# A four-layer graph network kernel: who keeps the block sums, who makes the spread matrix, and how GATv2's leaky logits are formed

## The reference, cut to what matters

```python
e = leaky_relu(xl[src] + xr[dst], 0.2)
logit = einsum('ehc,hc->eh', e, att)
a = exp(logit - segment_max(logit, dst)[dst])
out = segment_sum(a / segment_sum(a, dst)[dst] * xl[src], dst)
```

## Time and profile before

| | us |
|---|---|
| median of 3 runs | 8000.28 (7995.58 to 8005.35) |
| the profiled execution, its own time | 8003.79 |
| its span, first to last instruction | 8002.0 |
| sweep of GATv2, 128 wide (914 to 1566 us) | 652 |
| sweep of GATv2, 256 wide (1664 to 2487) | 823 |
| sweep of GAT (2670 to 3285) | 615 |
| three sweeps of the transformer | 682, 684, 682 |
| sweep of GIN (7106 to 7715) | 609 |

### The profile page before, as it was taken

How to read it: one execution, slowest core, us unless ns; L and a number is a source line. 1 busy time by engine, 2 the same in 40 slices (tenths; PEclk the granted TensorE clock), 3 DMA queues, 4 the chain that set the end, 5 groups by cost and what they waited for, 6 DMA issues and landing times. The chain is left out here.

```text
span 8002.0 us, 138934 instructions
## 1 busy us (share of the span) xinstructions
PE 5981.8 (75%) x30254; PEld 4761.3 (60%) x30255; DVE 5204.0 (65%) x17428; ACT 3151.4 (39%) x10642; POOL 3541.3 (44%) x3878
## 2 busy tenths in 40 slices
PE   2787577678886788497887897886887887937676
PEld 1665466657774566386665785665875665814455
DVE  7664488768887566538997328997338998353323
ACT  0111266646664466235553225553325553300015
POOL 0677366545552477306662006662006663037740
PEclk9999999899997688699998998998999998955678
DMA  1000211222222233326553026553026554023330
GB/s 29 3 3 3 55 48 48 39 74 73 72 74 40 79 102 102 62 101 187 175 177 84 2 94 185 176 174 96 0 89 180 176 177 104 0 82 100 101 68 16
DMA packets 306941, 689.93 MB, mean 86 GB/s; under 512 B 95900, under 2 KB 135510, under 8 KB 306390
## 3 DMA queue, kind: packets, MB, share of 16 engines
q0 software_dynamic: 209536, 581.61, 27.0%
q1 hardware_dynamic: 81264, 98.11, 3.8%
q10 hardware_dynamic: 15846, 7.19, 0.4%
HBM read 605.77 MB, written 80.89 MB: 86 GB/s over the span
## 5 line engine op out<-in xcount | busy, mean ns | idle before, releaser
L943 POOL DMA_INDIRECT arena<-tab_l,idx x2320 | 2203.7, 950 | 1032.6 <-issue 568.4
L1020 PE MATMUL bank<-arena,onehots 128*128 128x264 f32 (+3 forms) x6496 | 1980.6, 436 | 339.0 <-DVE onehots L852 189.4
L981 PE MATMUL bank<-arena,spreads 128*128 x5568 | 1458.6, 370 | 598.0 <-ACT spreads L1034 242.6
L1020 PEld LDWEIGHTS bank<-arena,onehots 128*128 128x128 f32 x6496 | 1312.1, 221 | 673.7 <-DVE onehots L852 211.9
L981 PEld LDWEIGHTS bank<-arena,spreads 128*128 128x128 f32 x5568 | 966.9, 206 | 827.7 <-issue 761.7
L1213 DVE TENSOR_TENSOR acc<-acc,bank 128x264 f32 (+3 forms) x1624 | 654.9, 403 | 498.2 <-PE bank L1020 486.7
L1034 ACT ACTIVATE spreads<-bank 128x256 f32<-128x256 f32 x1392 | 524.2, 377 | 900.6 <-PE bank L969 896.2
L1108 DVE TENSOR_TENSOR arena<-arena,bank 128x512 f32<-128x512 f32 x928 | 629.3, 680 | 265.9 <-ACT stats L1056 146.7
L861 ACT ACTIVATE onehots<-iota_row,slot_loc 128x128 f32<-128x128 f32 x1856 | 632.3, 391 | 28.6 <-PEq L1693 24.2
L943 POOL DMA_INDIRECT arena<-tab_l0b,idx x464 | 441.2, 951 | 374.9 <-ACT arena L1074 235.6
L930 POOL COPY idx<-slot_typed 128x16 int32 (+1 forms) x87 | 17.8, 204 | 1329.0 <-SPq L901 1328.6
(11 more groups left out here) (331 smaller groups left out, 9925.3 us busy)
## 6 DMA issues: line engine op xcount, KB each, us to landing
tab_l<-arena SPq DMA_DIRECT2D x75, 768.0 KB, 3.5
arena<-tab_l,idx POOLq DMA_INDIRECT x2320
arena<-tab_l0a,idx POOLq DMA_INDIRECT x464
arena<-tab_l0b,idx POOLq DMA_INDIRECT x464
rec_dram<-arena POOLq DMA_INDIRECT x417, 2.1
tab_l<-arena SPq DMA_DIRECT2D x25, 132.0 KB, 1.8
tab_l0b<-arena SPq DMA_DIRECT2D x25, 128.0 KB, 1.7
residual<-X SPq DMA_DIRECT2D x1, 3200.0 KB
```

The costliest lines, as they stand in the source:

```text
L943: pool.indirect_dma_start(out=rows_sb[:, a, t, 0:width], out_offset=None, in_=table[:, :], in_offset=bass.IndirectOffsetOnAxis(ap=idx[:, a ...
L981: mm = pe.matmul(z[x.k % 2][:, t, 0:cw], spreads[:, x.k % 2, t * P:t * P + P], qtab[:, block_no[w % BG], 0:cw], start=True, stop=not gatv2)
L1020: mm = pe.matmul(sums[x.k % 2], onehots[:, x.a, GT * x.k + t, :], rhs, start=t == 0, stop=t == GT - 1)
```

## The change

It has three parts, in the six softmax sweeps.

1. **Block sums.** The addition to `acc` leaves VectorE. TensorE adds the old sum with one more product, identity times the block's row of `acc` (L1020's accumulation goes on into it), and ScalarE copies the result from PSUM back to `acc` at lag 16. So the product of group g waits for ScalarE's copy of group g - 1 (`added_up`), and in a batch's first group for VectorE's rescaling, which moves from lag 16 to lag 15. TensorE reads two lists of block numbers a batch, ScalarE one, VectorE one. GIN keeps VectorE's addition.
2. **Spread matrix.** The two transposes and ScalarE's copy go. `load_slots` also writes the local slot numbers to DRAM in bf16 (four more transposes, one copy, four more stores). During a sweep SyncE's queue loads them, half a batch at a time (1024 numbers), broadcast to all partitions, into `loc_ring`, and VectorE compares four tiles at once with the partition number. That is one `tensor_scalar` of 128x512, bf16 in and fp32 out, for every two groups, at lag 0. The one-hots, now needed by the sums alone, are made at lag 4 (0 in GIN), and where VectorE makes them it is one `tensor_tensor` of 128x256 with broadcast operands.
3. **GATv2's leaky form.** 0.2 z + 0.8 max(z, 0). The part linear in z is projected beforehand: two more columns for each node (`lin`, 0.2 times weights times `att`), so tables and targets are 130 and 258 wide. z spans two PSUM banks a buffer. ScalarE copies 2x2 numbers in place of 0.2 z, and VectorE does one `scalar_tensor_tensor` (max with 0, times 0.8 `att`) and one `tensor_reduce`. The two parts meet once a batch, where the logits are collected.

The core of the diff:

```diff
+            dve.tensor_tensor(onehots[:, x.a, GT * x.k:GT * x.k + GT, :],
+                              iota_row[:, :].unsqueeze(1).to_broadcast(pair),
+                              loc[:, ds(BT * x.batch + GT * x.k, GT)].unsqueeze(2).to_broadcast(pair),
+                              ALU.is_equal).then_inc(S["oh_made"].sem, 1)
...
-            LAG = dict(one_hots=0, turn=1, target=2, logit=3, weigh=14, add_up=15, keep=16)
+            LAG = dict(spread=0, one_hots=4, target=2, logit=3, weigh=14, add_up=15, keep=16)
...
+                            sp.dma_start(loc_ring[:, h, :],
+                                         loc_dram[0:1, ds(BT * P * s + h * HALF, HALF)].to_broadcast([P, HALF]))\
+                              .then_inc(loc_in[h].sem, 16)
...
-                            pe.transpose(pot[x.k % 2][:, 0:P], onehots[:, x.a, GT * x.k, :], ident[:, :])
-                            pe.transpose(pot[x.k % 2][:, P:2 * P], onehots[:, x.a, GT * x.k + 1, :], ident[:, :])\
-                              .then_inc(S["oh_turned"].sem, 1)
...
+                            target_block = next_blocks(mybir.EngineType.PE, i, w, LAG["target"])
+                            sum_block = next_blocks(mybir.EngineType.PE, i, w, LAG["add_up"])
...
+                                if needed(x.g):
+                                    pe.wait_ge(S["added_up"].sem, S["added_up"].at(x.g))
+                                if x.k == 0:
+                                    pe.wait_ge(S["rescaled"].sem, S["rescaled"].at(x.batch + 1))
+                                mm = pe.matmul(sums[x.k % 2], ident[:, :], acc[:, sum_block[w % BG], 0:wc],
+                                               start=False, stop=True)
...
+                            act.wait_ge(S["summed"].sem, S["summed"].at(x.g + 1))
+                            act.activation(acc[:, keep_block[w % BG], 0:wc], sums[x.k % 2], ACT.Copy)\
+                               .then_inc(S["added_up"].sem, 1)
...
-                            act.activation(rows_sb[:, x.a, GT * x.k:GT * x.k + GT, D:D + cw], z[x.k % 2][:, :, 0:cw],
-                                           ACT.Copy, scale=0.2)\
-                               .then_inc(S["activated"].sem, 1)
...
+                            dve.tensor_scalar(spread_ring[:, quad % 2, :],
+                                              loc_ring[:, h, quad % 2 * 4 * P:quad % 2 * 4 * P + 4 * P],
+                                              small[:, 0:1], None, ALU.is_equal).then_inc(S["spread_made"].sem, 1)
...
-                            dve.tensor_tensor(pr, pr, src[:, :, D:D + cw], ALU.max).then_inc(S["leaked"].sem, 1)
+                            dve.scalar_tensor_tensor(pr, pr, 0.0, att[:, 0:width].unsqueeze(1)
+                                                     .to_broadcast([P, GT, width]), ALU.max, ALU.mult)\
+                               .then_inc(S["multiplied_rows"].sem, 1)
...
-                                    op = dve.tensor_tensor_reduce(
-                                        out=z[xl.k % 2][:, t, ch], in0=z[xl.k % 2][:, t, ch], in1=att[:, ch],
-                                        scale=1.0, scalar=0.0, op0=ALU.mult, op1=ALU.add,
-                                        accum_out=r[:, t, h:h + 1])
+                            dve.tensor_reduce(r, lane_split(pr, width // 2), AX, ALU.add)\
+                               .then_inc(S["raw_made"].sem, 1)
...
-                            dve.tensor_tensor(av, av, sums[x.k % 2], ALU.add).then_inc(S["added_up"].sem, 1)
...
+                        if lin is not None:
+                            for k in range(kb):
+                                pe.matmul(lins[a], xT[:, a, k * P:k * P + P], lin[:, k, :], start=k == 0,
+                                          stop=k == kb - 1)
...
+            vector_phase(slopes(128, 2, 0))
...
+            vector_phase(slopes(256, 1, 256))
```

More of the change, by code:

```diff
@@ L42 @@
 LH = 64
+HALF = BT * P // 2
+ARENA = 26752
 assert (P - 1) * EC < E and NB % 2 == 1 and NT % 2 == 1 and GRP <= NB * BG
@@ L1272, in edge_pass @@
                 S["mid"].base += NB * 9
+                S["spread_made"].base += NB * 4
+                for h in range(2):
+                    loc_in[h].base += 16 * NB
             if gatv2:
-                per_group += ("activated", "leaked")
+                per_group += ("activated", "multiplied_rows")
             if hgt:
```

216 lines of the change are left out of this document (132 added, 84 removed).

## The result

The changed kernel takes 8903.32 us (median of 4 runs, 8896.33 to 8905.71), the kernel before 8002.82 us (4 runs, 7995.58 to 8008.28): a ratio of 1.112, 95% interval 1.1105 to 1.1144. It is 11% slower. The forecast was 7950 us, between 7825 and 8060.

What follows compares the result with a forecast made beforehand. Different limits bind by stage: GpSimd's gathers (floor 21.0 us a batch), VectorE in the transformer, TensorE in wide GATv2. Terms -61 + 17 - 43 + 36 = -51 us from 8003.8 gave 7953, stated as 7950 us, range 7825 to 8060.

Steps and rivals of the forecast that it cites:

- The second list of block numbers: Wide GATv2 sweep: TensorE's added read costs 0 to 0.7 us a batch; 0.3 taken, as TensorE's queue is full.
- rival C: TensorE pays, identity product and second read stay bare: +78 us wide GATv2, +26 transformer, 8097 us in all; chance 0.18.
- The claim that VectorE's work hides TensorE's: Transformer sweeps: TensorE's added 0.22 us a group is hidden by VectorE's 2.6; bare it would be 1.8 a batch.
- The transformer, -61 us forecast: Three transformer sweeps: -1.0 - 0.2 + 0.5 = -0.7 us a batch, -61 us; at best -218, at worst +35.
- rival D: Transformer: the mixed comparison goes at the single rate, 755 ns, +1.1 us a batch, +93 us, 8045 us; chance 0.07.
- VectorE's relief: Transformer sweeps: VectorE loses 2.6 us a batch of additions and gains 1.6 of comparisons, net -1.0 us a batch.
- the chain from the weights: Transformer: summing products, then ScalarE's copy to `acc`, then first weighing; VectorE's wait of 1.3 us a batch grows by 0.5.
- The wide GATv2 sweep, +17 forecast: TensorE's work grows 2.0 us a batch, its idle time falls 1.4, from 3.7 to 2.3: +17 us, bounds -9 and +78.
- rival B: VectorE's relief counts more in the transformer and wide GATv2 (-9 us in the latter), about 7820 us in all; chance 0.22.
- The narrow one, -43 forecast: Narrow GATv2 sweep falls 1.5 us a batch to GpSimd's floor of 21.0: -43 us, bounds -45 and 0.
- rival E: VectorE's comparisons delay GpSimd's gathers in GAT and narrow GATv2, +110 us, 8060 us in all; chance 0.04.
- GAT and outside: GAT, already on GpSimd's floor: 0, 6 either way. Additions outside the sweeps (projection, `slopes`, `load_slots`): +36 us, 20 to 60.

Runs made afterwards that it cites:

- TensorE's lists on the boundary: The changed kernel with TensorE's two lists and ScalarE's aligned, VectorE's read still off the boundary: 8213.21 us, 1.0258 of the kernel before.
- second_read_behind: The changed kernel with all lists aligned and TensorE's second read moved behind the batch's first target products: 8024.86 us, 1.003 of the kernel before.
- sums_in_gatv2_alone: second_read_behind with the first part undone in GAT and the transformer and kept in GATv2: 8001.78 us, 1.0002 of the kernel before.
- no_identity: The changed kernel without the identity product; the build also dropped its second read: 0.9771 of the kernel before, second kind of chip.
- sums_undone: The changed kernel with the first part undone, comparison and GATv2's split form kept, lists not aligned: 0.9665 of the kernel before, second kind of chip.
- after_again: The changed kernel as it is, run again as yardstick on the second kind of chip: 1.0375 of the kernel before.
- sums_undone_quick: The changed kernel with the first part undone and the remaining reads on the boundary: 0.964 of the kernel before, second kind of chip.
- before_two_reads: The kernel before with a second, unused TensorE read, which the build dropped, leaving the kernel before: ratio 0.9997, second kind of chip.

## Why the prediction was wrong

Sweeps in us on the first kind of chip, from first to last gather. The forecast is the length before plus the forecast's term; outside is the span less the seven sweeps.

| | before | forecast | changed | TensorE's lists on the boundary | second read behind | first part in GATv2 alone |
|---|---|---|---|---|---|---|
| GATv2, narrow | 649.5 | 607 | 699.6 | 634.5 | 629.4 | 630.4 |
| GATv2, wide | 820.2 | 837 | 905.1 | 796.4 | 775.6 | 774.8 |
| GAT | 612.0 | 612 | 767.9 | 631.8 | 621.2 | 618.2 |
| transformer, each | 680 | 659 | 859 | 744 | 692 | 685 |
| GIN | 606.4 | 606 | 611.6 | 608.9 | 608.9 | 608.6 |
| outside | 3275 | 3311 | 3334 | 3314 | 3310 | 3309 |

**The step that failed** is "The second list of block numbers costs between 0 and 0.7 us a batch, the gap at such a read being 0.69; I take 0.3", which was besides put into the wide sweep's sum alone. The read of the earlier trace rows starts on the boundary, and the row puts its gap down to ScalarE's copy, not to the read. The change dropped the moved copy of the list, so it made TensorE's existing read, the new one and VectorE's three times as long. The full diff shows this, and the forecast gave it no cost. The upper bound should have been 2 x 1.94 less 0.59, 3.3 us a batch in all six sweeps, plus the half clock behind it: 5.4 us in the batch above, with its measured gap. That is in kind rival C's mechanism, "Identity product and second read stay bare", at five times its size: C had 0.7 us a batch for the read and 0.3 for the slow clock behind it. Its chance was 0.18, and it stopped at 8097.

The claim that VectorE's work hides TensorE's failed with it. "TensorE gains 0.22 us a group, which VectorE's 2.6 us a group hide" is true of 0.22 us spread over slots; it is not true of 3.8 us in one piece ahead of products for which VectorE waits: those waits are 131.9 us of a sweep of the changed kernel.

```profile
DVE bank L1180 <- PE bank L1009: 131.9, 29, 5.1
```

**With quick reads the forecast would still have been off.** second_read_behind takes 8025 us where the kernel before takes 8001. That lies within the stated range, but it is 24 us slower where 51 us faster were forecast, and misses cancel in it: the transformer came out 99 us above its term and the wide GATv2 sweep 62 us below its own.

**The transformer, -61 us forecast, +38 with quick reads** (693.3, 694.3 and 689.4 us against 679.2, 680.5 and 679.2). The comparison was sized rightly: its median is 479 ns where 473 was worked out, so it goes at the double rate from bf16 (rival D is out):

```profile
L1161 DVE TENSOR_SCALAR arena<-arena,small x696: 470/479/726, 928.4 to 7581.5; 128x512 f32<-128x512 bf16 x174
```

VectorE's relief was right in the main too: 597 us busy against 619, 22 of the 29 us that were forecast. What failed is that the relief becomes idle time, 96 us of 693. The waits of second_read_behind in that sweep say where:

```profile
DVE arena L1150 <- ACT stats L1098: 36.8, 26, 2.7
...
DVE arena L1150 <- PE bank L1059: 26.9, 27, 2.2
PE bank L1059 <- DVE acc L1262: 23.1, 27, 1.0
...
DVE bank L1183 <- PE bank L1010: 13.1, 26, 1.9
```

The weighing's wait went from 38.8 us a sweep to 63.7, so from 1.3 to 2.2 us a batch, where 1.8 was forecast. But it did not grow at `stats` (33.2 before, 36.8 now). It grew at TensorE's sums, from 5.5 to 26.9: the weighing (L1150) waits 1.0 us a batch for the identity product (L1059), which itself waits 0.9 us for VectorE's rescaling (L1262). `summed`, on which the weighing waits for its buffer, now also includes the old sum. The forecast followed the chain from the weights and not the one over the buffer. The last row is new as well: for 13 us VectorE's product with the keys waits for TensorE's target products, a wait that the kernel before does not show in this sweep.

Without the first part in this sweep (sums_in_gatv2_alone) VectorE has its additions back, and the weighing waits 7.7 us in all:

```profile
DVE arena L1150 <- PE bank L1051: 7.7, 12, 1.1
```

So the first part takes 62 us of work off VectorE (659 to 597) and gives back 56 us of waits at the weighing and 8 at the product with the keys, and the sweep is some 7 us longer with it (685 to 692). That the wait for the identity product is the cause of it, and not the clock (0.91 without, 0.96 with) or the new copy on ScalarE, is inferred from these rows, not tried.

**The wide GATv2 sweep, +17 forecast, -45 with quick reads.** "TensorE over 92% busy" came true: 721 of 776 us, 93%. But its clock is 0.99, not 0.97, and its idle time fell to 54 us, 1.9 a batch where 2.3 was expected, while 2.0 us a batch of added work came out as 0.2 (721.5 against 714.5 busy, over slightly different stretches). The relief was worth more than its stated sum: rival B's direction for this sweep, at five times its -9 us.

**The narrow one, -43 forecast, -20 measured**, stops at 629 us and not at GpSimd's floor of 607. GpSimd is busy 458 us there, not 447: its gathers take longer. The changed kernel's page shows it for the wide and the narrow sweep:

```profile
L976 POOL DMA_INDIRECT arena<-tab_l0b,idx x464 | 464.8, 1002 | 436.2 <-DVE raw L1238 188.7
...
L976 POOL DMA_INDIRECT arena<-tab_l0a,idx x464 | 458.5, 988 | 236.9 <-issue 108.7
```

In the kernel before both were 951 ns, and in GAT and the transformer GpSimd's busy time grew by only 3 and 7 us a sweep. The direction is rival E's: 11 us of the narrow sweep where its rule made it 55. The Trainium skill, SBUF — State Buffer, "Who interferes with whom", calls VectorE's two-port modes an exclusive lock against GpSimd; the trace shows a few per cent on each gather. Not all of it is the comparison, which all six sweeps have. In the wide sweep a gather takes 968 ns without the identity product (no_identity) and 965 with the first part undone (sums_undone), 1000 in after_again, so most of its excess came with the first part; in the narrow one these runs leave it at 979 and 985, and there the rows of the table, now 130 numbers, are an untested rival. In the transformer it takes 958 ns with the comparison on ScalarE and 972 with it on VectorE (sums_undone_quick).

**GAT and outside.** Forecast 0 and +36, measured +9 and +35 with quick reads. The sums of small records along the projection and `load_slots` held. Two slips in the forecast's arithmetic change nothing in this: the transformer's worst case comes to +0.3 us a batch by its own terms, +26 and not +35, and rival D's +93 on 7950 is 8043, not 8045.

**What stays open.** VectorE's read off the boundary and the place of the second read together make 188 us on the first kind of chip; they were not parted. That long reads alone would make the loss in the kernel before was not seen: two of them were run in it on the second kind only, and gave 1.007 to 1.011 there, with the same gap of 3.9 us, where the changed kernel gains 5.2% by quick reads (VectorE's among them). So there the loss takes both, the long reads and something else of the change; what, was not tried. Nor is it known why one such read made the kernel before's two GATv2 sweeps faster there.

## What to carry to other kernels

Price an instruction by the addresses it touches, not by its name: a line of a diff that only tidies a table up can change every read of it. Let a read of registers from SBUF start at a multiple of 16 bytes, and keep a moved copy of the table for each lag if it takes that. Put such a read behind work that is already queued: here TensorE's stall cost 3.1 us more in a batch and the half clock behind it another 2.3. Work that moves to another engine also moves into the semaphores that already count it, so follow every wait on them, the ones for buffers too.

## What the runs showed of the hardware

- **A read of eight 4-byte numbers into registers** takes 0.59 us on TensorE, 0.60 on VectorE and 0.55 on ScalarE when it starts at a multiple of 16 bytes, and 1.94, 1.85 and 1.75 us when it starts 4 or 8 bytes past one. On the boundary, starts at a multiple of 32 bytes were tried on all three engines, and 16 bytes past such a multiple on TensorE alone (0.59 us). The Trainium skill, DMA: Bandwidth & Descriptors, "Latency and other measured facts", gives `tensor_load` a floor of some 600 ns; the records on the boundary agree on TensorE, 592 ns, and ScalarE's 548 lie a little below. The Trainium skill, Advanced Engine Details and Errata, "SBUF Cachelines", gives lines of 16 bytes, the boundary found here. By such lines a read of 32 bytes off the boundary touches three in place of two; that alone is half as many again, and the measured factor is over three.
- **Two kinds of chip.** The same kernel takes 8000 or 9420 to 9530 us, and the operations take the same time on both: a gather 948 to 951 ns (mean of a sweep) on the first and 947 to 955 on the second, the weighing 680 and 682. On the second kind the engines stop together at times while the DMA goes on. Three stretches of a transformer sweep of before_two_reads, which is the kernel before (busy time of PE, PEld, DVE, ACT and POOL, then clock, DMA share and GB/s):

```profile
4578.00:4580.00 2.00, 1.28 (x6) 0.76 (x4) 0.04 (x1) 0.00 (x0) 1.57 (x2) 1.00 0.78 215
4580.00:4582.00 2.00, 0.00 (x0) 0.00 (x0) 0.66 (x1) 0.00 (x0) 0.95 (x1) 1.00 0.72 217
4582.00:4584.00 2.00, 0.00 (x0) 0.00 (x0) 1.16 (x2) 1.09 (x4) 0.00 (x0) 1.00 0.44 133
```

After a gather that ends at 4581.1 no engine is busy until VectorE and ScalarE start again at 4582.84 and 4582.88. By the code both wait there for signals that go back to TensorE's products, and its last product before that began at 4578.2. The page of before_two_reads puts 836 us of ScalarE's waits down to a releaser that it cannot see:

```profile
L1035 ACT ACTIVATE spreads<-bank 128x256 f32<-128x256 f32 x1392 | 525.0, 377 | 1861.9 <-remote 835.9
```

Whether the signals or the products are late was not found, and no run here shows what differs between the chips. But a comparison can turn over between the two kinds: the first part undone, with the comparison and the split form kept, is 3.4% faster than before on the second kind, and on the first the nearest version is level with it.
